# Cross attention in three rounded products, with the softmax's division moved behind the weighting

## The reference

```python
q = _rms_norm((draft_hidden @ Wq.T).reshape(b, s, H, HD), q_norm_w)
kv_in = jnp.concatenate([context_hidden, draft_hidden], axis=1)
k = _rms_norm((kv_in @ Wk.T).reshape(b, total, KVH, HD), k_norm_w)
v = (kv_in @ Wv.T).reshape(b, total, KVH, HD)
q, k = _rope(q, draft_position_ids), _rope(k, full_position_ids)
scores = jnp.einsum('bhqd,bhkd->bhqk', q, k) * SCALE
probs = jax.nn.softmax(scores, axis=-1)
attn = jnp.einsum('bhqk,bhkd->bhqd', probs, v)
return attn.reshape(b, s, H * HD) @ Wo.T
```

## Time and profile before

| | us |
|---|---|
| median of three runs | 2493.8 (2493.62 to 2494.19) |
| the profiled execution's own time | 2492.17 |
| its span (first to last instruction) | 2490.5 |
| TensorE busy, over the span | 2181.5 (88%) |
| VectorE, ScalarE, GpSimd busy | 1309.4, 1020.9, 887.9 |
| first to last score of cross attention | 1079.8 to 1952.2 |

### The profile page before, as it was taken

How to read it: one execution, slowest core, us unless ns; L and a number is a source line. 1 busy time by engine, 2 the same in 40 slices (tenths; PEclk the granted TensorE clock), 3 DMA queues, 4 the chain that set the end, 5 groups by cost and what they waited for, 6 DMA issues and landing times. The chain is left out here.

```text
span 2490.5 us, 35704 instructions
## 1 busy us (share of the span) xinstructions
PE 2181.5 (88%) x10448; PEld 1664.9 (67%) x10448; DVE 1309.4 (53%) x2830; ACT 1020.9 (41%) x2184; POOL 887.9 (36%) x906
## 2 busy tenths in 40 slices
PE   5689999995789989599999999999999799749991
PEld 3578888874577777366666666666666588637771
DVE  3635555555766666444454545454555256535554
ACT  2313333333344444345555555555555322125660
POOL 2400000002555555534232323323235255446664
PEclk8889999997899999799999999999999999869996
DMA  7621211134344444332222222222221344154336
GB/s 284 170 71 38 67 36 61 38 109 142 105 123 123 126 128 151 113 110 73 66 58 65 74 58 77 58 65 58 65 58 38 92 114 118 51 198 135 101 106 194
DMA packets 289858, 243.77 MB, mean 98 GB/s; under 512 B 147842, under 2 KB 254834, under 8 KB 286322
## 3 DMA queue, kind: packets, MB, share of 16 engines
q1 hardware_dynamic: 269122, 190.19, 26.0%
q10 hardware_dynamic: 14160, 34.22, 3.8%
q0 software_dynamic: 6496, 18.37, 2.8%
HBM read 149.31 MB, written 93.42 MB: 97 GB/s over the span
## 5 line engine op out<-in xcount | busy, mean ns | idle before, releaser
L2234 DVE TENSOR_REDUCE ca_down<-ca_ps_s 112x1 f32<-112x487 f32 x256 | 164.6, 661 | 308.5 <-PE ca_ps_s L2047 306.4
L1971 POOL TENSOR_TENSOR ca_k<-ca_k 125x512 f32<-125x512 f32 x64 | 81.2, 1269 | 541.4 <-DVE ca_k L2219 541.4
L2047 PE MATMUL ca_ps_s<-ca_kT,ca_qT 128*112 128x487 f32 x512 | 230.5, 572 | 0.8 <-issue 0.8
L2136 ACT ACTIVATE ca_prob<-ca_ps_s,ca_down 112x487 f32<-112x487 f32 x256 | 169.8, 666 | 135.2 <-DVE ca_down L2234 131.1
L75 PE MATMUL out_ps_y<-out_w_hi,out_o_hi 128*128 128x512 f32 x448 | 189.2, 422 | 33.7 <-DVE out_w_lo L1288 18.9
L2063 PE MATMUL ca_ps_o<-ca_pT,ca_v 125*128 125x448 f32 (+1 forms) x512 | 203.2, 539 | 0.6 <-ACT ca_pT L2143 0.6
L75 PE MATMUL ca_ps_p<-ca_w_hi,ca_c_hi 128*125 128x512 f32 x384 | 174.0, 453 | 23.1 <-POOL ca_c_lo L1965 23.1
L76 PE MATMUL out_ps_y<-out_w_lo,out_o_hi 128*128 128x512 f32 x448 | 182.1, 406 | 0.0
L77 PE MATMUL out_ps_y<-out_w_hi,out_o_lo 128*128 128x512 f32 x448 | 181.6, 405 | 0.0
L599 POOL COPY sa_val<-lat_v 112x128 f32<-112x128 f32 (+1 forms) x64 | 18.9, 296 | 411.2 <-PE sa_ps_o L656 410.9
L2063 PEld LDWEIGHTS ca_ps_o<-ca_pT,ca_v 125*128 125x128 f32 (+1 forms) x512 | 97.1, 190 | 100.9 <-issue 100.1
(11 more groups left out here) (291 smaller groups left out, 5671.5 us busy)
## 6 DMA issues: line engine op xcount, KB each, us to landing
self_outT<-sa_ov SPq DMA_DIRECT2D x64, 224.0 KB, 2.4
out_o_raw<-self_outT SPq DMA_DIRECT2D x56, 256.0 KB, 3.0
cross_qT<-out_qt SPq DMA_DIRECT2D x56, 256.0 KB, 2.5
ca_qT<-cross_qT SPq DMA_DIRECT2D x64, 224.0 KB, 2.8
cross_outT<-ca_ov SPq DMA_DIRECT2D x64, 224.0 KB, 3.0
out_o_raw<-cross_outT SPq DMA_DIRECT2D x56, 256.0 KB
ffn_raw<-in_expert_w SPq DMA_DIRECT2D x8, 1536.0 KB, 7.0
ca_c_first<-in_ctxT SPq DMA_DIRECT2D x15, 750.0 KB
```

The costliest lines, as they stand in the source:

```text
L1971: pool.tensor_tensor(k1[0:m, :], k1[0:m, :], k2[0:m, :], ALU.add).then_inc(k_added.sem, 1)
L2047: pe.matmul(ps_s[j % 2][:, :], qT[i % 2][:, j, :], kT[par][:, i, :], start=True, stop=True).then_inc(scored.sem, 1)
L2136: act.activation(prob[j][:, 0:KV], ps_s[j % 2][:, :], ACT.Exp, bias=down[:, j:j + 1], accum_out=total[:, j:j + 1]).then_inc(exped.sem, 1)
L2234: dve.tensor_reduce(down[:, j:j + 1], ps_s[j % 2][:, :], AX.X, ALU.max, negate=True).then_inc(maxed.sem, 1)
```

## The change

It has four parts. Scores and weighting become `mm3`: keys, queries, values and transposed probabilities are each split into a high part (ScalarE, a rounding copy) and a low part (VectorE; for queries GpSimd). Keys get a 488th column, so a score has an even width. The division goes: the exponentials are transposed and weighted as they are, and VectorE multiplies the output by the inverse sums (`scale_o`). The sums belong to query rows, which are partitions, while the output has queries along its free dimension; so the inverse sums of a step (112 partitions x 4) are written to memory and read back to all 128 partitions by SP (`turn_sums`). Room is made: two tiles of probabilities for four, one transposed tile for two, and the high output weights of six heads only, so ten heads are split at the start of `cross_output` by ScalarE and VectorE.

```diff
+            def turn_sums(b, i):
+                rows = sums[i * HQ:(i + 1) * HQ, bass.ds(b * S, S)]
+                wait(sp, inverted, b, i)
+                carry(sp, b, ticks)
+                sp.dma_start(rows.rearrange("h q -> q h"), inv[i % 2][:, :], allow_slow_non_contiguous=True).then_inc(inv_put[i % 2].sem, 16)
+                wait(sp, inv_put[i % 2], b, i // 2)
+                carry(sp, b, ticks)
+                sp.dma_start(inv_all[i % 2][:, :, :], rows.unsqueeze(0).broadcast_to((P, HQ, S))).then_inc(inv_in[i % 2].sem, 16)
...
                 if more > 1:
                     load(b + 2, h + 1, par)
+                turn_sums(b, 0)
                 load_q(b, 3)
                 store(b, 0)
                 if more > 1:
                     load_ctx(b + 2)
+                turn_sums(b, 1)
                 if more:
                     load_q(b + 1, 0)
                 store(b, 1)
+                turn_sums(b, 2)
                 if more:
                     load_q(b + 1, 1)
                 store(b, 2)
+                turn_sums(b, 3)
...
+            def low_q(b, i):
+                wait(pool, q_hi_ready, b, i)
+                pool.tensor_tensor(q_lo[i % 2][:, :, :], q_raw[i % 2][:, :, :], q_hi[i % 2][:, :, :], ALU.subtract)\
+                    .then_inc(q_lo_ready.sem, 1)
...
             def score(b, h, i, j, par):
                 if j == 0:
-                    wait(pe, q_in[i % 2], b, i // 2)
+                    wait(pe, q_lo_ready, b, i)
                     if i == 0:
                         wait(pe, kT_ready, b, 3)
                 wait(pe, exped, b, i * HQ + j - 2)
-                pe.matmul(ps_s[j % 2][:, :], qT[i % 2][:, j, :], kT[par][:, i, :], start=True, stop=True).then_inc(scored.sem, 1)
+                mm3(pe, ps_s[j % 2][:, :], q_hi[i % 2][:, j, :], q_lo[i % 2][:, j, :], kT_hi[par][:, i, :],
+                    kT_lo[par][:, i, :], True, True).then_inc(scored.sem, 1)
...
             def turn(b, i, j):
                 n = i * HQ + j
-                wait(pe, probs, b, n)
+                wait(pe, exped, b, n)
                 wait(pe, pT_ready, b, n - 2)
...
             def weigh(b, i, par):
...
                 wait(pe, o_ready, b, i - 1)
                 for t in range(4):
-                    mm = pe.matmul(ps_o[:, :, :], v[par][0:M[t], t, i * HD:(i + 1) * HD], pT[i % 2][0:M[t], t, :, :],
-                                   start=(t == 0), stop=(t == 3))
+                    m, d = M[t], slice(i * HD, (i + 1) * HD)
+                    mm = mm3(pe, ps_o[:, :, :], v_hi[par][0:m, t, d], v_lo[par][0:m, t, d], pT_hi[0:m, t, :, :],
+                             pT_lo[0:m, t, :, :], t == 0, t == 3)
...
             def step(b, h, i, par, more):
                 score(b, h, i, 0, par)
                 score(b, h, i, 1, par)
+                if more:
+                    values(b + 1, i, 1 - par)
                 if begun(b, i):
                     pb, pi = before(b, i)
                     weigh(pb, pi, par if i else 1 - par)
-                if more:
-                    values(b + 1, i, 1 - par)
...
+            for tile in kT_hi + kT_lo:
+                act.activation(tile[:, :, KV], ident[:, 0:KVH], ACT.Copy)
...
+            def invert(b, i):
+                wait(dve, exped, b, i * HQ + HQ - 1)
+                if not isinstance(b, int) or b or i > 1:
+                    wait(dve, inv_put[i % 2], b, i // 2 - 1)
+                    carry(dve, b, dve_ticks)
+                dve.reciprocal(inv[i % 2][:, :], total[:, :]).then_inc(inverted.sem, 1)
+
+            def scale_o(b, i):
+                wait(dve, pv, b, i)
+                wait(dve, o_put[i % 2], b, i // 2 - 1)
+                wait(dve, inv_in[i % 2], b, i // 2)
+                dve.tensor_tensor(ov[i % 2][:, :, :], ps_o[:, :, :], inv_all[i % 2][:, :, :], ALU.mult).then_inc(o_ready.sem, 1)
...
             for par in range(2):
                 body(par, 0, par)
-            for t in range(2):
-                for c in range(NQ):
-                    high(t, c)
+            high(0, 0)
+            high(0, 1)
+            for c in range(1, NQ):
+                for h in range(max(c * HQ, READY), (c + 1) * HQ):
+                    split(h)
+                if c > 1:
+                    high(0, c)
+            for c in range(NQ):
+                high(1, c)
```

More of the change, by code:

```diff
@@ L1699, in body @@
                     locate(t - 2, par)
+            for h in range(READY, H):
+                dve.wait_ge(w_hi_ready, h - READY + 1)
+                dve.tensor_tensor(w_lo[:, h, :], w_raw[:, h, :], w_hi[h], ALU.subtract).then_inc(w_lo_ready, 1)
             dve.wait_ge(r_src, 32)
@@ L1777, in cross_output, with cross_attention @@
     return ctx
-def cross_attention(nc, ahead_of, ctxT, xT_hi, xT_lo, tables, qT_src, oT, next_w):
+def cross_attention(nc, ahead_of, ctxT, xT_hi, xT_lo, tables, qT_src, sums, oT, next_w):
     M = (CT, CT, CT, S)
@@ L1815, in cross_attention @@
         ps_p = [ctx.bank(f"ps_p{i}", P, D) for i in range(2)]
-        ps_s = [ctx.bank(f"ps_s{i}", S, KV) for i in range(2)]
+        ps_s = [ctx.bank(f"ps_s{i}", S, KV + 1) for i in range(2)]
         ps_t = [ctx.bank(f"ps_t{i}", P, 4, S) for i in range(2)]
@@ L1843, in cross_attention @@
         exped = ev("exped", N, 2)
-        inverted = ev("inverted", N)
-        probs = ev("probs", N)
-        p_turned = ev("p_turned", N, HQ)
-        pT_ready = ev("pT_ready", N, 2)
-        pv = ev("weighted", 4, 2)
+        inverted = ev("inverted", 4)
+        inv_put = [ev(f"inverse_stored{i}", 2, 1, 16) for i in range(2)]
+        inv_in = [ev(f"inverse_loaded{i}", 2, step=16) for i in range(2)]
+        p_turned = ev("p_turned", N, 2)
+        pT_hi_ready = ev("pT_hi", N)
+        pT_ready = ev("pT_lo", N, 2)
+        pv = ev("weighted", 4, 1)
         o_ready = ev("o_ready", 4, 1)
@@ L1957, in _ @@
             k_scaled.open(pool)
-            for j in range(HQ):
+            for j in range(2):
                 pool.memset(prob[j][:, KV:4 * CT], 0.0).then_inc(padded, 1)
@@ L1981, in project @@
                     low(b + 1, 0, 1 - par)
+                if queries:
+                    low_q(*queries)
             def step(b, h, i, par, more):
                 if more:
-                    project(b + 1, i, 1 - par)
-                if isinstance(b, int) and b:
-                    first = {1: i, B - 2: HQ + i, B - 1: 2 * (HQ + i)}[b]
-                    for head in range(first, first + (2 if b == B - 1 else 1)):
+                    project(b + 1, i, 1 - par, after(b, i))
+                elif i < 3:
+                    low_q(b, i + 1)
+                if isinstance(b, int) and b in (1, B - 2):
+                    head = i if b == 1 else HQ + i
+                    if head < next_w.READY:
                         next_w.split(pool, head)
             low(0, 0, 0)
-            batches(pool, project, step)
+            batches(pool, project, step, lambda: low_q(0, 0))
         @block.tensor
@@ L2134, in exp @@
                 wait(act, maxed, b, n)
-                wait(act, p_turned, b, n - HQ)
-                act.activation(prob[j][:, 0:KV], ps_s[j % 2][:, :], ACT.Exp, bias=down[:, j:j + 1],
+                wait(act, p_turned, b, n - 2)
+                if j == 0 and (not isinstance(b, int) or b or i):
+                    wait(act, inverted, b, i - 1)
+                act.activation(prob[j % 2][:, 0:KV], ps_s[j % 2][:, 0:KV], ACT.Exp, bias=down[:, j:j + 1],
                                accum_out=total[:, j:j + 1]).then_inc(exped.sem, 1)
@@ L2173, in step @@
                     next_high(nb, i, npar)
-                if begun(b, i):
-                    copy_o(*before(b, i))
                 if more:
                     keep_v(nb, i, npar)
+                if more or i < 3:
+                    high_q(*after(b, i))
                 copy_pT(b, i, 0)
@@ L2198, in _ @@
             square(0, 0)
-            batches(act, start, step)
-            copy_o(B - 1, 3)
+            batches(act, start, step, lambda: high_q(0, 0))
         @block.vector
@@ L2254, in step @@
                     rotate(b + 1, h + par, i, 1 - par)
+                if begun(b, i):
+                    pb, pi = before(b, i)
+                    low_p(pb, pi, 2)
+                    low_p(pb, pi, 3)
                 maximum(b, i, 0)
@@ L2258, in step @@
                     squares(b + 1, i)
-                divide(b, i, 0)
-                divide(b, i, 1)
+                if more:
+                    low_v(b + 1, i, 1 - par)
+                if begun(b, i):
+                    scale_o(pb, pi)
                 maximum(b, i, 2)
+                low_p(b, i, 0)
                 maximum(b, i, 3)
-                divide(b, i, 2)
-                divide(b, i, 3)
+                low_p(b, i, 1)
+                invert(b, i)
+                if more:
+                    low_k(b + 1, i, 1 - par)
             for n in range(2):
@@ L2664, in build @@
     qT = dram("cross_qT", (P, H, T))
```

(3 more changed lines are left out.)

106 lines of the change are left out of this document (70 added, 36 removed).

## The result

The changed kernel takes 2614.4 us (median of four runs, 2611.4 to 2627.8) against 2493.7 us for the kernel before on the same chip: a ratio of 1.0494, 95% interval 1.0458 to 1.0531. It is slower, where the prediction said 2434 us and faster. The number is that of rival 3, the round trip of the inverse sums. Times and ratios compare fast executions with fast ones; one execution of experiment 12 (5319.8 us) and one of experiment 9 (2861.8), which nothing here explains, are left out of both.

What follows compares the result with a forecast made beforehand. TensorE's own work was taken to bound the third from 1080 to 1905 us; -69.6 + 2 + 6.6 + 1.2 + 0.5 = -59.3 us gave a median of 2434 us. Forecast range 2428 to 2442, wider range 2426 to 2462.

Steps and rivals of the forecast that it cites:

- rival 3: Loop: the round trip becomes the step; at D = 12 steps last 15.7 us, kernel about 2615; chance 0.05.
- D: Inverse sums' round trip through memory: write 2.8, read 2.8, semaphores and issue 0.5; 6.1 us, bounds 4.9 and 10.2.
- The queueing: Batch's first step: sums queue on SP behind big loads, 0.1 us late on 14 batches; 2 us allowed.
- rival 1: Loop: 1 to 3 us stalls behind big loads, or D between 7.5 and 9: 2445 to 2465 us; chance 0.2.
- TensorE's saving: Loop step: scores save 0.61 us, weighting 0.56, from 13.97 to 12.80 us; 69.6 us over 60 steps.
- rival 2: Loop: new products cost as 512 columns, or TensorE pauses at order changes; 0.72 us saved per step, 2461; chance 0.08.
- Do the others keep up: Loop step: VectorE 9.2 of 12.8 us, ScalarE exchanges copies, GpSimd adds 1.1 on 4.5; none is a bound.
- When the scaling is wanted: Loop: sums land 4.5 us into next step, wanted at 6.65; slack 2.2 us, 3 until TensorE feels it.
- the ring: Loop: D + 3.7 us (scaling to next reciprocal) must pass every step; TensorE sets the pace up to D = 9.1.
- Start of the stage: Stage start: fills 1.2 us, three steps' key copies and subtractions 3.7, queries' rounding and subtraction 1.7; +6.6 us.
- Last batch: Last batch: steps from 10.09 to 9.7 us, four giving -1.0; output after last transposes +2.2; total +1.2 us.
- Output projection: Output projection: ten head splits on ScalarE and VectorE finish two to five us ahead of use; +0.5 us.

Runs made afterwards that it cites:

- experiment 12: Changed kernel with the 448 sums written 64 B apart and the read fetching rotation table rows instead (wrong scaling): 2439.4 us, ratio 0.9817.
- experiment 9: Changed kernel with the same write, but the read fetching four old rows of the rotation tables (wrong scaling): 2643.8 us, ratio 1.0626.
- experiment 2: Changed kernel with sums laid out contiguously: write 112 pieces of 16 B, read one piece of 1792 B a partition; 2429.2 us, ratio 0.9749.
- experiment 1: Changed kernel without both transfers of the sums, output multiplied by constant ones (not normalised): 2433.1 us, ratio 0.9774.
- experiment 5: Changed kernel with contiguous sums and the output's scaling moved behind the inversion and low keys on VectorE: 2423.9 us, ratio 0.9741.
- experiment 8: Changed kernel with the deferred division undone: exponentials divided on VectorE head by head, output copied, no trip; 2430.2 us, ratio 0.9765.
- experiment 7: Changed kernel writing one head's 112 sums instead of 448 and reading that row for all four heads: 2921.8 us, ratio 1.1754.
- experiment 6: Changed kernel with the read as one piece of 1792 B a partition, the write still 448 single floats: 2604.2 us, ratio 1.0481.

## Why the prediction was wrong, point by point

**The step that failed** is the price of the inverse sums' round trip, D = 6.1 us. "Write: ... I take 2.8" measured 6.3 to 6.9, and "Read: same 512 pieces of 448 bytes as a load of queries, 2.8 us" measured 4.1. In a light step D is 11.0 us, above even the upper bound of 9.1 that TensorE can hide and above the 10.2 that I called the worst. The bound failed because its rows didn't have the property that costs. The write's upper bound, 5.1 us, was an indirect write of 128 numbers; no row of the trace wrote 4-byte pieces side by side at such a number. Its lower bound, the 1.7 us of the 1 KB list, was a load and not a write at all. The read's price came from a transfer with the same number and size of pieces but distinct sources. The 5.0 us that the prediction worked out from the Trainium skill, DMA: Bandwidth & Descriptors, section Anatomy of one DMA, rests on a fit that the page gives for transfers issued by GpSimd; SP issued these, and D measured 11.0 us in the light steps.

**The queueing** behind the tables (rival 1's matter, +2 us) had its direction right: the write waits 2.7 us longer in a batch's first step (9.44 against 6.70) and 0.7 in the second. On top of a trip without slack this costs in full. With the quick trip of experiment 2 it is hidden all but 34.4 us of VectorE's waiting, none of which shows in the mean step of 12.79.

**TensorE's saving**: right. 12.80 us were predicted for a step, 12.79 measured in experiments 1, 2, 5 and 8. Products of 488 columns follow each other in 0.22 us and of 448 in 0.20, and the granted clock is 0.99 to 1.00 over those loops. This is why rival 2 falls. The clock of 0.94 in the changed kernel's loop comes with the gaps of TensorE; as the step is the trip plus 3.3 us of VectorE and ScalarE, no part of the loss needs it.

**Do the others keep up**: right, experiments 1 and 8 show it, even with the division on VectorE (660 us busy of 805). **When the scaling is wanted**: the cycle beyond D was taken as 3.7 us and is 3.3; the ring was rightly named. **Start of the stage**: +6.6 us predicted. The first score starts 5.6 us later in experiment 1, 6.4 in experiment 2 and 8.1 in the changed kernel than before (1079.82 us); right to within 1.5 us. **Last batch**: with the trip away its steps are 8.9 us, from 10.09 in the earlier trace rows; with the quick trip 9.2 to 11.3, where 9.7 was predicted, up to 1.6 too little. **Output projection**: the time from the last scaling to the first product is 9.9 to 10.3 us in experiments 1 and 2, 9.95 in the changed kernel and 9.83 before; +0.5 was right.

**Rival 3** said: at D = 12 a step of 15.7 and 2615 us. The mean D was 12.1 (14.40, 11.87, 11.01, 11.07), the mean step 15.40 and the time 2614.4. That its total came out so close is in part luck: 0.3 us a step too much, some 18 us over 60 steps, made up for start and end, which were given 20 us and took about 35 (an estimate: the loss of 120.7 less 60 steps of 15.40 - 13.97). Where the 180.2 us between the spans of the changed kernel and experiment 1 lie, from their reciprocals: 125.3 in the 48 steps of batches 2 to 13 (48 x (15.40 - 12.79)), 15.2 in the first batch, 12.5 in batches 1 and 14, 21.3 in the last batch, 5.0 between its last reciprocal and the last scaling, 2.5 ahead of the first reciprocal. That is 181.8; what stands behind the last scaling took 1.6 less in the changed kernel.

Rival 1 was also added wrong: its own terms (15 to 30 us and 8) give 2457 to 2472, not 2445 to 2465. Nothing measured turns on it.

The chance of 0.05 for rival 3 was too small by the prediction's own argument. It had two unpriced operations in series, a slack of 3 us over a priced 6.1, and a rule that spoke against them. The Trainium skill, DMA: Bandwidth & Descriptors, section Specifications, says that below 512 B the engines read, modify and write. The runs agree that a write of 4-byte pieces can be slow (6.9 us in the changed kernel) but don't show that mechanism: at the same size it takes from 2.6 to 6.5 us as the pieces lie, and 512 stores of 448 B, below that size too, land in 2.4 us. The same page, section Rules for kernel authors, says that a strided last dimension becomes one descriptor per element and should be made contiguous. That advice is worth 185 us here (experiment 2 against the changed kernel). The number of pieces alone doesn't account for it: a quarter of them took as long (experiment 7), and all 448 spread out took less than half (experiment 12).

**Left open**: why close writes complete so late, and over which unit of memory (16, 4 and 1 floats in 64 B give 6.5, 3.6 and 2.6 us; no wider spacing was tried, nor the same spacing with neighbours from different partitions); why the same one-piece read lands in 3.3 us in experiment 2 and in 4.1 in experiment 6; and why old table rows (4.8) read slower than fresh sums (4.1). None of it changes where the loss lies.

## What to carry to other kernels

Price a transfer from a row whose pieces have not only the same number and size but the same neighbours: for a write, how close the pieces lie; for a read, how many partitions want the same bytes. When an unpriced round trip stands in a ring with a slack of half its price, the ring is the forecast to beat, and its law (trip plus what follows it until the next trip can start) gives the step of the bad case; here it held within 0.03 us over six kernels. And lay scratch memory out as it stands on chip: contiguous 16 B per partition made a loss of 4.9% a gain of 2.5%.

## What the runs showed of the hardware

- 448 single floats written side by side (four rows of 112) take 6.5 to 7.0 us to land, 112 of them 6.9; 16 B apart 3.6, 64 B apart 2.6. In the cycle shown, the DMA engines are idle in 4.63 of the write's 6.33 us. With an empty queue the same 1792 B in pieces of 16 B let SP go on after 1.55 us.
- Reading 224 KB in 512 pieces of 448 B takes 2.8 to 3.1 us if the pieces are distinct, 4.1 to 4.8 if 128 partitions share each of four rows, and 8.2 to 9.3 if all share one. Behind the last, another load is held up too (queries 5.2 to 6.7 us instead of 2.8).
- VectorE's scaling takes 0.97 us where the factors are read with a stride of four floats (experiment 2), 0.625 us where they are contiguous.
